# Other loads and orders of the first batches, row transposes in halves, and up1 of batch 30 behind h of batch 31, in an attention and experts kernel

## The chip, the cores and the metric

The kernel runs on one core of one Trainium2 chip. The metric is device time in microseconds (us) of one execution. Engines: PE (TensorE; PEld is its weight load), DVE (VectorE), ACT (ScalarE), POOL (GpSimd) and SP (SyncE, which here only issues DMAs).

## What is computed

Shapes: x and ctx are 32 batches of 128 channels by 1024 positions. Each batch goes through cross attention with a sliding window of 16 keys and 8 heads of 16 channels, and then, per row of 1024, through a mixture of 8 rank-64 experts of which the best two count.

```
x1  = x + Wo @ attn(q = Wq @ layernorm(x) + bq, k = Wk @ ctx + bk, v = Wv @ ctx + bv) + bo
      # position t attends to keys t-8 .. t+7
p   = softmax(layernorm(x1) @ gate_w.T); the two largest, divided by their sum -> w_full
out = x1 + sum over e of w_full[:, e] * (layernorm(x1) @ lora_A[e].T) @ lora_B[e].T
```

Rows are the 128 channels of a batch: layernorm runs along the 1024 positions, and the four projections mix channels.

## The kernel before

Weights stay in SBUF. Every operand of a large product is kept as two fp32r parts, `[:, 0]` ("hi", written by ACT) and `[:, 1]` ("lo", what is left, written by POOL or DVE), and `product` and `project_pass` (through `one_pass`, line 366) make three matmuls of them: hi-hi, hi-lo, lo-hi. Scores (line 395, 32x32 pieces), weighted values (line 416, 64x64 pieces) and transposes (line 425) are plain fp32.

The order is written out by hand for each engine: `head`, then `step` 30 times, then `tail`. A step works on several batches: `later` and `ahead` (loads, layernorm, projections of the next ones), `cur` (scores and softmax, in 4 chunks), `prev` (weighted values, output projection, residual and second layernorm) and `old` (the experts). On PE a step is, in order: project_v(cur), weighted chunk 2 of prev, 8 transposes of the normalised rows of old into the two banks of `bank_a`, score chunk 1, project_q(ahead), the down product of old in four quarters with a weighted or score chunk behind each, project_k(ahead), score chunk 3, 4 transposes of h, project_o(prev), weighted chunk 1 of cur, the up product of old in two halves (called up0 and up1 here) with score chunk 0 of ahead between.

The transposed rows are evacuated by ACT (`rows_hi`, line 718) and DVE (`rows_lo`, line 1005) in two halves, one after each four transposes. A transpose takes 128 columns of a row block and writes 128 columns of one bank:

```
for f in blocks:
    last = nc.tensor.transpose(bank[:, f * P:(f + 1) * P],
                               source[:, f * P:(f + 1) * P], ident[:])
```

`raw` is one buffer for x and ctx of a batch in turn. SP loads x into it, ACT writes the normalised x over it, POOL takes the lo part from it (`normal_lo`, line 1217), then SP loads ctx into it; ACT and POOL split that too (`context_hi`, line 723, `context_lo`, line 1194). In the head, ctx of batches 0 and 1 have places of their own (`prob_t`, `xn2`), but x of batch 1 waits for `normal_lo` of batch 0. The nine pieces of the weights are loaded in the head into buffers that are free then, and split by ACT (`split_hi`) and POOL or DVE (`split_lo`, lines 1181 and 876). The first two masks are written into `bank_b` by PE (`first_masks`, line 361), later ones by ACT (`write_mask`, line 683). `warm_up` runs 60 small matmuls ahead of all.

In the tail, batches 30 (`old`) and 31 (`last`) are finished: h transposes of 30, row transposes of 31, up of 30, down of 31, h transposes of 31, up of 31.

Of the kernel before, what the change touches and what calls it, by code (L numbers as in the profile page):

```python
# [36 lines left out]
P = 128  # L37
# [61 lines left out]
def build(nc, x, ctx, wqkvo, biases, down_w, up_w, ident_in, mask_in, consts_in, out):  # L99
    with ExitStack() as stack:  # L100
# [61 lines left out]
        weights_hi, weights_lo = sem("weights_hi"), sem("weights_lo")  # L162
# [4 lines left out]
        x_in, ctx_in = sem("x_in"), [sem("ctx_in0"), sem("ctx_in1")]  # L167
# [44 lines left out]

        def ctx_of(b):

            if isinstance(b.j, int) and b.c <= 1:
                return (prob_t[:, 0:T], xn2[:])[b.c]
            return raw[:]

        def ffn_bank(b):

            return bank_c if isinstance(b.j, int) and b.j == 0 and b.c == BATCHES - 1 else bank_a

# [28 lines left out]
        def _(sp):  # L251
# [16 lines left out]
            def load_x(b):  # L268

                row = b.row(sp)  # L270
                if b.c >= 1:
                    sp.wait_ge(xn_lo, b.count(1, 0))
                if b.c >= 3:
                    sp.wait_ge(ctx_lo, b.count(1, 0))
                sp.dma_start(raw[:], x[row]).then_inc(x_in, 16)

            def load_ctx(b):

                row = b.row(sp)
                if b.c >= 2:  # L280
                    sp.wait_ge(xn_lo, b.count(1, 1))
                sp.dma_start(ctx_of(b), ctx[row]).then_inc(ctx_in[b.parity], 16)

            def load_resid(b):
# [4 lines left out]
                else:  # L289
                    sp.wait_ge(weights_lo, 6 + b.c)  # L290
# [8 lines left out]
            def head(b0, b1, b2, b3):  # L299

                load_x(b0)
                load_ctx(b0)
                sp.dma_start(consts[:], consts_in).then_inc(consts_in_sbuf, 16)
                load_piece(0)
                load_piece(1)
                sp.dma_start(bias[:], biases).then_inc(small_in, 16)
                sp.dma_start(ident[:], ident_in).then_inc(small_in, 16)
                sp.dma_start(mask[:], mask_in).then_inc(small_in, 16)
                load_piece(2)
                load_piece(3)  # L310
                load_piece(4)
                load_piece(5)
                load_piece(6)
                load_piece(7)
                load_ctx(b1)
                load_piece(8)
                load_x(b1)
                place_v(b0)
                load_x(b2)
                load_resid(b0)  # L320
                load_ctx(b2)
# [33 lines left out]
        def _(pe):  # L355
            def first_masks():
# [3 lines left out]
                for m in range(2):  # L360
                    nc.tensor.matmul(bank_b[m][:], ident[:], mask[:], start=True, stop=False, skip_group_check=True)
# [59 lines left out]

            def transposes(bank, source, blocks):
# [15 lines left out]
            def up(b, n, e):  # L438

                last = product(ffn_bank(b)[:, n * HALF:(n + 1) * HALF], ht_split,  # L440
# [6 lines left out]
            def bank_of(b):  # L447

                return bank_a if first(b) else bank_c

            def project_q(b, free):

                pe.wait_ge(xn_done, b.count(1, 1))
                pe.wait_ge(xn_lo, b.count(1, 1))
# [871 lines left out]
```

## Time and profile before

| | us |
|---|---|
| three runs | 1031.46, 1033.31, 1034.66 |
| median | 1033.31 |
| the profiled execution | 1032.37 |
| its span, first to last instruction | 1030.6 |
| busy in the span: PE / PEld / DVE / ACT / POOL | 997.1 / 861.7 / 867.1 / 582.2 / 433.5 |
| mean granted TensorE clock, of full speed | 0.987 |

The span is what the trace covers; 1.8 us of the profiled execution lie around it. Busy times of different engines overlap. PE's matmuls are pipelined and their ends are modelled, so the distance from one group's start to the next one's start is the better measure of what it costs; the rows give starts. A granted clock of 1.0 is 2.4 GHz, 0.5 is 1.2 GHz.

### The profile page before, as it was taken

The numbers are of one execution on the slowest core, as the hardware profiler recorded it, in microseconds if no ns is written. First come the engines' busy times: TensorE is split into PE (matmuls) and PEld (weight loads), VectorE is DVE, ScalarE is ACT, GpSimd is POOL, SyncE is SP. The second block draws the span as 40 slices with busy tenths as digits, with TensorE's granted clock in tenths as the row PEclk, the third lists the DMA queues.
The fourth block names the chain that finished last, engine by engine and source line by source line (L and its number), as shares of the span: only waits on it lengthen the run. The fifth ranks groups of instructions, "written<-read, shape, count | busy, mean of one in ns | idle before, by whom it ended". The sixth has DMA issues, their size and how long they took to land.

```text
span 1030.6 us, 54778 instructions
## 1 busy us (share of the span) xinstructions
PE 997.1 (97%) x24572; PEld 861.7 (84%) x24572; DVE 867.1 (84%) x1889; ACT 582.2 (56%) x812; POOL 433.5 (42%) x373
## 2 busy tenths in 40 slices
PE   6779999999999999999999999999999999999987
PEld 5658888888888888888888888888888888888876
DVE  2778888898888898988898888889888889898872
ACT  6766555555555565555566555556555556565330
POOL 6864434343434444434444443434443434443220
PEclk8899999999999999999999999999999999999998
DMA  7323333312333322333322333331233332232211
GB/s 270 87 67 83 86 106 106 104 54 77 87 104 106 106 61 89 86 85 106 106 64 85 86 85 106 106 90 66 79 86 105 106 104 59 92 85 66 65 42 41
DMA packets 157866, 92.49 MB, mean 90 GB/s; under 512 B 139744, under 2 KB 139872, under 8 KB 157664
## 3 DMA queue, kind: packets, MB, share of 16 engines
q1 hardware_dynamic: 157664, 89.25, 29.6%
q8 instruction: 193, 3.16, 1.3%
q14 instruction: 9, 0.07, 0.0%
HBM read 55.16 MB, written 16.78 MB: 70 GB/s over the span
## 4 chain that ended last, share of the span: by engine, by line
PE 92%; DMA 2%; DVE 2%; ACT 1%; issue 1%; POOL 1%; DVEq 0%; POOLq 0%
PE bank_a L366 36%; PE bank_c L366 18%; PE bank_b L416 18%; PE bank_b L395 15%; PE bank_a L425 5%; DMA raw<-x 1%; DMA raw<-ctx 1%; DVE stats L886 0%; POOL x_split L1217 0%; POOL ctx_split L1194 0%; DVE resid_pair L1025 0%; ACT q_diag L693 0%; ACT v_sb L710 0%; ACT ctx_split L723 0%; POOL rstd L1202 0%
## 5 line engine op out<-in xcount | busy, mean ns | idle before, releaser
L416 PEld LDWEIGHTS bank_b<-prob_t,v_diag 64*64 64x64 f32 x4608 | 188.4, 133 | 33.0 <-issue 24.6
L366 PE MATMUL bank_a<-down_split,mid_split 128*128 128x264 f32 (+1 forms) x1488 | 207.6, 289 | 2.3 <-DVE mid_split L1005 2.2
L1188 POOL TENSOR_TENSOR prob<-prob,row_inv 128x512 f32<-128x512 f32 x128 | 134.3, 1050 | 169.0 <-DVE row_inv L975 169.0
L416 PE MATMUL bank_b<-prob_t,v_diag 64*64 64x96 f32 (+2 forms) x4608 | 202.6, 239 | 0.0
L366 PEld LDWEIGHTS bank_a<-down_split,mid_split 128*128 128x128 f32 x1488 | 187.6, 188 | 9.2 <-DVE mid_split L1005 2.9
L395 PEld LDWEIGHTS bank_b<-k_sb,q_diag 32*32 32x32 f32 x16384 | 155.2, 105 | 44.6 <-issue 36.5
L366 PE MATMUL bank_a<-up_split,ht_split 128*128 128x512 f32 x744 | 187.5, 401 | 0.3 <-DVE ht_split L1012 0.3
L395 PE MATMUL bank_b<-k_sb,q_diag 32*32 32x32 f32 x16384 | 170.5, 194 | 11.8 <-issue 7.7
L366 PEld LDWEIGHTS bank_a<-up_split,ht_split 128*128 128x128 f32 x744 | 135.9, 189 | 29.4 <-DVE ht_split L1012 0.7
L1211 POOL TENSOR_TENSOR attn_split<-attn,attn_split 128x1024 fp32r<-128x1024 f32 x32 | 76.1, 2377 | 139.7 <-ACT attn_split L730 139.7
L984 DVE STREAM_TRANSPOSE prob_t<-prob 128x768 f32<-128x768 f32 x128 | 121.5, 950 | 0.9 <-POOL prob L1188 0.9
L678 ACT ACTIVATE prob<-prob 128x512 f32<-128x512 f32 x128 | 80.2, 626 | 58.6 <-DVE prob L963 58.6
L672 ACT ACTIVATE attn<-bank_b,consts 128x256 f32<-128x256 f32 x128 | 59.5, 465 | 85.6 <-PE bank_b L416 85.6
L366 PE MATMUL bank_c<-ctx_split,w_split 128*128 128x512 f32 x372 | 98.5, 400 | 4.3 <-POOL ctx_split L1194 4.3
L1217 POOL TENSOR_TENSOR x_split<-raw,x_split 128x1024 fp32r<-128x1024 f32 x32 | 77.0, 2406 | 60.7 <-ACT raw L742 60.7
L1194 POOL TENSOR_TENSOR ctx_split<-raw,ctx_split 128x1024 fp32r<-128x1024 f32 x30 | 72.0, 2400 | 61.1 <-ACT ctx_split L723 61.1
L963 DVE TENSOR_TENSOR prob<-bank_b,row_max 128x512 f32<-128x512 f32 x128 | 88.5, 691 | 4.4
L957 DVE TENSOR_REDUCE row_max<-bank_b 128x16 f32<-128x512 f32 x128 | 85.0, 664 | 7.5 <-PE bank_b L395 7.2
L1202 POOL TENSOR_TENSOR rstd<-var_eps,consts 128x1 f32<-128x1 f32 x64 | 35.1, 549 | 132.1 <-DVE var_eps L895 132.1
L971 DVE TENSOR_REDUCE row_sum<-prob 128x16 f32<-128x512 f32 x128 | 85.2, 666 | 0.5 <-ACT prob L678 0.3
L905 DVE SCALAR_TENSOR_TENSOR attn<-bank_b,consts,attn 128x256 f32<-128x256 f32 x128 | 58.3, 458 | 31.2 <-ACT attn L672 31.2
L366 PEld LDWEIGHTS bank_c<-ctx_split,w_split 128*128 128x128 f32 x372 | 68.6, 191 | 17.7 <-issue 4.4
(94 smaller groups left out, 1334.4 us busy)
## 6 DMA issues: line engine op xcount, KB each, us to landing
v_diag<-v_t SPq DMA_DIRECT2D x128, 132.0 KB, 3.3
raw<-x SPq DMA_DIRECT2D x32, 512.0 KB, 5.2
resid_pair<-x SPq DMA_DIRECT2D x32, 512.0 KB, 4.8
out<-resid_pair SPq DMA_DIRECT2D x31, 512.0 KB, 2.6
raw<-ctx SPq DMA_DIRECT2D x30, 512.0 KB, 3.2
stage<-down_w SPq DMA_DIRECT2D x2, 528.0 KB, 11.4
q_diag<-up_w SPq DMA_DIRECT2D x2, 512.0 KB, 6.2
prob_t<-up_w SPq DMA_DIRECT2D x2, 512.0 KB, 8.4
```

What stands on the lines that cost most here:

```text
L366: return nc.tensor.matmul(dst, st[:, s, st_cols], mv[:, m, mv_cols], start=start and n == 0, stop=stop and n == 2)
L395: last = nc.tensor.matmul(bank_b[m % 2][rows, t * KT:(t + 1) * KT], q_diag[rows, cur.parity, n, :], keys[rows, n * QT:n * QT + KT], start= ...
L416: last = nc.tensor.matmul(bank_b[2 + m % 2][rows, lo * PW:hi * PW], value_blocks(b)[rows, n, :], prob_t[rows, at:at + (hi - lo) * KT], sta ...
L678: nc.scalar.activation(weights_of(m), weights_of(m), ACT.Exp).then_inc(exp_done, 1)
L957: nc.vector.tensor_reduce(row_max[:, cols], scores, AX_X, ALU.max).then_inc(max_done, 1)
L963: nc.vector.tensor_tensor(weights_of(m), scores, row_max[:, cols].unsqueeze(2).broadcast_to([P, CT, KT]), ALU.subtract).then_inc(shifted, 1)
L971: nc.vector.tensor_reduce(row_sum[:, cols], weights_of(m), AX_X, ALU.add).then_inc(sum_done, 1)
L984: nc.vector.transpose(prob_t[:, m * PC:(m + 1) * PC], prob[:, m % 2 * PC:(m % 2 + 1) * PC]).then_inc(prob_t_done, 1)
L1188: nc.gpsimd.tensor_tensor(weights_of(m), weights_of(m), row_inv[:, cols].unsqueeze(2).broadcast_to([P, CT, KT]), ALU.mult).then_inc(prob_d ...
L1194: nc.gpsimd.tensor_tensor(ctx_split[:, 1, :], ctx_of(b), ctx_split[:, 0, :].bitcast(F32), ALU.subtract).then_inc(ctx_lo, 1)
L1211: nc.gpsimd.tensor_tensor(attn_split[:, 1, :], attn[:], attn_split[:, 0, :].bitcast(F32), ALU.subtract).then_inc(attn_lo, 1)
L1217: nc.gpsimd.tensor_tensor(x_split[:, 1, :], raw[:], x_split[:, 0, :].bitcast(F32), ALU.subtract).then_inc(xn_lo, 1)
```

## The change

It has three parts.

**The first batches.** Batch 0's projections are single fp32 matmuls of the unsplit weights and operands (`project_first`), so no hi and lo parts are made for it; x of batch 1 is loaded into the place of `k_sb[1]`, x of batch 2 into `raw` once q of batch 0 is projected, ctx of batch 2 into `xn2`; the DMAs are issued in another order; the two first masks are written one by one; `warm_up` has 34 matmuls, and a `keep_warm` of 28 stands before score chunk 2 of batch 0; pieces 1 to 3 of the weights are split by DVE; and the orders of PE, ACT, DVE and POOL in the head differ. Semaphores of the weights' lo parts become one for each piece.

**Row transposes.** Sixteen in place of eight, each of 64 rows of `xn2` (the lower half into bank 0 of the pair, the upper into bank 1), alternating. `rows_hi` and `rows_lo` take a bank at a time, that is 64 rows of all eight blocks, ACT and DVE do both halves in a row, and the down product waits for both before its first quarter.

**Tail.** up1 of batch 30 stands behind the h transposes of batch 31; the inner parts of batch 31 go to `w_split`, so that those of batch 30 stay.

```
-                if b.c >= 1:
-                    sp.wait_ge(xn_lo, b.count(1, 0))
-                if b.c >= 3:
-                    sp.wait_ge(ctx_lo, b.count(1, 0))
-                sp.dma_start(raw[:], x[row]).then_inc(x_in, 16)
+                if early(b) and b.c == 2:
+                    sp.wait_ge(q_done, 1)
+                elif not early(b):
+                    sp.wait_ge(xn_lo, b.count(1, -1))
+                    sp.wait_ge(ctx_lo, b.count(1, -1))
+                sp.dma_start(x_of(b), x[row]).then_inc(first_x[b.c] if early(b) else x_in, 16)
...
+            def row_transposes(bank):
+
+                for f in range(FK):
+                    for z in range(HALVES):
+                        rows = slice(z * HALF_P, (z + 1) * HALF_P)
+                        at = z * HALF + f * HALF_P
+                        last = nc.tensor.transpose(bank[:, at:at + HALF_P], xn2[rows, f * P:(f + 1) * P],
+                                                   ident[rows, rows])
+                        if f == FK - 1:
+                            last.then_inc(xt_done, 1)
...
+            def project_first(bank, which, source):
+
+                for n in range(2):
+                    half = slice(n * HALF, (n + 1) * HALF)
+                    last = nc.tensor.matmul(bank[:, half], attn[:, which * P:(which + 1) * P],
+                                            source[:, half], start=True, stop=True)
+                return last
...
-                pe.wait_ge(xt_lo, old.count(2, 1))
+                pe.wait_ge(xt_lo, old.count(2, 2))
...
                 pe.wait_ge(ht_lo, old.count(1, 1))
-                for n in range(2):
-                    for e in range(EK):
-                        up(old, n, e)
+                for e in range(EK):
+                    up(old, 0, e)
                 pe.wait_ge(xt_lo, last.count(2, 2))
                 for n in range(2):
                     for f in range(FK):
                         down(last, n, f)
                 pe.wait_ge(h_done, last.count(2, 2))
                 transposes(bank_c, h_sb, range(EK)).then_inc(ht_done, 1)
+                for e in range(EK):
+                    up(old, 1, e)
                 pe.wait_ge(ht_lo, last.count(1, 1))
...
                 if old:
                     rows_lo(old, 0)
+                    rows_lo(old, 1)
                 if cur:
                     scores_shift(cur, 1)
                     weights_transpose(cur, 0)
-                if old:
-                    rows_lo(old, 1)
-                if cur:
                     weights_sum(cur, 1)
```

SP's DMAs in the head from the mask's on, before (up_w and down_w are pieces 1 to 8 of the weights, xn is `xn2`; x and ctx of batch 0 and piece 0 are issued ahead of these rows, in both kernels):

```order
L308 DMA mask<-mask_in 128x512
L254 DMA q_diag<-up_w 128x1024
L254 DMA prob_t<-up_w 128x1024 x2
L254 DMA resid_pair<-down_w 128x1024 x2
L254 DMA stage<-down_w 128x1056
L282 DMA xn<-ctx 128x1024
L254 DMA stage<-down_w 128x1056
L275 DMA raw<-x 128x1024
```

And now:

```order
L331 DMA mask<-mask_in 128x512
L275 DMA q_diag<-up_w 128x1024
L297 DMA k_sb<-x 128x1024
L306 DMA xn<-ctx 128x1024
L275 DMA q_diag<-up_w 128x1024
L275 DMA prob_t<-up_w 128x1024 x2
L275 DMA resid_pair<-down_w 128x1024
L297 DMA raw<-x 128x1024
L275 DMA resid_pair<-down_w 128x1024
L275 DMA stage<-down_w 128x1056
L286 DMA v_diag<-v_t 32x33x32 x4
L306 DMA xn<-ctx 128x1024
```

x of batch 1 stood behind all pieces of the weights, its ctx behind all but one; now both (k_sb<-x, xn<-ctx) go ahead of seven of the nine, and x of batch 2 (the second raw<-x) ahead of the last three.

PE at the start of the head, before:

```order
L496 MATMUL bank_c<-prob 32x32 x60
L361 MATMUL bank_b<-mask,ident 128x512 x2
L366 MATMUL bank_a<-ctx_split,w_split 128x512 x6
L366 MATMUL bank_c<-x_split,w_split 128x512 x6
L366 MATMUL bank_a<-ctx_split,w_split 128x512 x6
L395 MATMUL bank_b<-k_sb,q_diag 32x32 x192
L366 MATMUL bank_c<-x_split,w_split 128x512 x6
L395 MATMUL bank_b<-k_sb,q_diag 32x32 x64
```

And now (attn is the unsplit piece of the attention weights, prob_t is ctx of batch 0, raw its normalised x; L548 is `keep_warm`):

```order
L543 MATMUL bank_b<-prob 32x32 x34
L485 MATMUL bank_a<-prob_t,attn 128x512 x2
L485 MATMUL bank_c<-raw,attn 128x512 x2
L384 MATMUL bank_b<-mask,ident 128x512
L485 MATMUL bank_a<-prob_t,attn 128x512 x2
L418 MATMUL bank_b<-k_sb,q_diag 32x32 x64
L384 MATMUL bank_b<-mask,ident 128x512
L418 MATMUL bank_b<-k_sb,q_diag 32x32 x64
L548 MATMUL bank_b<-ident 32x32 x28
L418 MATMUL bank_b<-k_sb,q_diag 32x32 x64
L389 MATMUL bank_c<-x_split,w_split 128x512 x6
L418 MATMUL bank_b<-k_sb,q_diag 32x32 x64
```

The three projections of batch 0 are six instructions in place of eighteen and take no split part, and one mask stands behind the first score chunk.

PE at the end of the tail, before (bank_a is batch 30, bank_c batch 31):

```order
L425 MATMUL bank_a<-ident,h_sb 128x128 x4
L425 MATMUL bank_c<-ident,xn 128x128 x8
L366 MATMUL bank_a<-up_split,ht_split 128x512 x24
L366 MATMUL bank_c<-down_split,mid_split 128x264 x24
L366 MATMUL bank_c<-down_split,mid_split 128x256 x24
L425 MATMUL bank_c<-ident,h_sb 128x128 x4
L366 MATMUL bank_c<-up_split,ht_split 128x512 x24
```

And now:

```order
L459 MATMUL bank_a<-ident,h_sb 128x128 x4
L451 MATMUL bank_c<-ident,xn 128x64 x16
L389 MATMUL bank_a<-up_split,ht_split 128x512 x12
L389 MATMUL bank_c<-down_split,mid_split 128x264 x24
L389 MATMUL bank_c<-down_split,mid_split 128x256 x24
L459 MATMUL bank_c<-ident,h_sb 128x128 x4
L389 MATMUL bank_a<-up_split,ht_split 128x512 x12
L389 MATMUL bank_c<-up_split,w_split 128x512 x24
```

Twelve of the 24 matmuls of up of batch 30 stand between the h transposes and the up product of batch 31, which reads its stationary operand from w_split.

## Rows read from the trace of the kernel before

**Rows 1.** The page: busy time, share of the span and instructions of each engine

```profile
PE 997.1 (97%) x24572; PEld 861.7 (84%) x24572; DVE 867.1 (84%) x1889; ACT 582.2 (56%) x812; POOL 433.5 (42%) x373
```

**Rows 2.** Windows: from:to, length, busy by engine, PEclk (granted clock), DMA share, GB/s

```profile
150.00:950.00 800.00, 798.71 (x20005) 692.23 (x20005) 707.68 (x1540) 466.50 (x652) 334.21 (x287) 1.00 0.31 88
1021.00:1022.00 1.00, 1.00 (x4) 0.79 (x3) 0.00 (x0) 0.00 (x0) 0.00 (x0) 0.50 0.00 0
```

**Rows 3.** Timeline of PE, one steady step: start, length, instructions

```profile
500.93 1.56 PE L366 MATMUL bank_c<-ctx_split,w_split 128*128 128x512 f32 x6
502.42 1.58 PE L416 MATMUL bank_b<-prob_t,v_diag 64*64 64x64 f32 x36
503.92 1.09 PE L425 MATMUL bank_a<-ident,xn 128*128 128x128 f32 x8
504.94 1.41 PE L395 MATMUL bank_b<-k_sb,q_diag 32*32 32x32 f32 x128
...
507.79 1.61 PE L366 MATMUL bank_a<-down_split,mid_split 128*128 128x264 f32 x12
...
521.03 0.66 PE L425 MATMUL bank_a<-ident,h_sb 128*128 128x128 f32 x4
521.44 1.63 PE L366 MATMUL bank_c<-attn_split,w_split 128*128 128x512 f32 x6
...
528.67 3.01 PE L366 MATMUL bank_a<-up_split,ht_split 128*128 128x512 f32 x12
531.53 1.56 PE L366 MATMUL bank_c<-ctx_split,w_split 128*128 128x512 f32 x6
```

**Rows 4.** Groups by form: busy us, mean ns of one, idle before

```profile
L416 PEld LDWEIGHTS bank_b<-prob_t,v_diag 64*64 64x64 f32 x4608 | 188.4, 133 | 33.0 <-issue 24.6
...
L366 PEld LDWEIGHTS bank_c<-ctx_split,w_split 128*128 128x128 f32 x372 | 68.6, 191 | 17.7 <-issue 4.4
...
L425 PEld LDWEIGHTS bank_a<-ident,xn 128*128 128x128 f32 x248 | 26.5, 140 | 1.6 <-ACT xn L749 0.4
```

**Rows 5.** Timeline of DVE in that step, first lo part of the transposed rows

```profile
505.82 0.65 DVE L1005 TENSOR_TENSOR mid_split<-bank_a,mid_split 128x512 fp32r<-128x512 f32 x1
```

**Rows 6.** Timeline of PE, head and start of the first step

```profile
9.58 1.96 PE L361 MATMUL bank_b<-mask,ident 128*128 128x512 f32 x4 [1.27 <-DMA mask<-mask_in]
...
12.79 1.63 PE L366 MATMUL bank_c<-x_split,w_split 128*128 128x512 f32 x6
...
19.67 2.99 PE L395 MATMUL bank_b<-k_sb,q_diag 32*32 32x32 f32 x207 [1.06 <-ACT q_diag L693]
...
29.80 2.21 PE L366 MATMUL bank_c<-x_split,w_split 128*128 128x512 f32 x6
...
58.90 2.90 PE L366 MATMUL bank_c<-ctx_split,w_split 128*128 128x512 f32 x6 [4.32 <-POOL ctx_split L1194]
...
68.34 1.66 PE L366 MATMUL bank_c<-ctx_split,w_split 128*128 128x512 f32 x6
```

**Rows 7.** Chain that ended last, in order of time, first 80 us

```profile
10.30 2.40 POOL x_split L1217
...
12.72 9.05 DMA raw<-x
```

**Rows 8.** Timeline of DVE, head: lo part of the attention weights

```profile
7.99 2.05 DVE L876 TENSOR_TENSOR w_split<-attn,w_split 128x512 fp32r<-128x512 f32 x1 [1.72 <-ACT w_split L655]
```

**Rows 9.** Timeline of ACT, head

```profile
7.87 1.23 ACT L742 ACTIVATE x_split<-raw,shift,rstd 128x1024 fp32r<-128x1024 f32 x1
...
17.23 2.29 ACT L693 ACTIVATE q_diag<-bank_c,bq_scaled,consts 128x1024 f32<-128x1024 f32 x2
19.41 1.12 ACT L710 ACTIVATE v_sb<-bank_a,bias 128x1024 f32<-128x1024 f32 x1
```

**Rows 10.** Timeline of PE, end of the tail

```profile
1017.98 0.66 PE L425 MATMUL bank_c<-ident,h_sb 128*128 128x128 f32 x4 [0.58 <-DVE h_sb L946]
1020.05 7.32 PE L366 MATMUL bank_c<-up_split,ht_split 128*128 128x512 f32 x24 [1.41 <-DVE ht_split L1012]
```

More of the change, by code:

```diff
@@ L161, in build @@
         weights_in = [sem(f"weights_in{n}") for n in range(9)]
[L162 removed]
+        weights_hi = sem("weights_hi")
+        weights_lo = [sem(f"weights_lo{n}") for n in range(9)]
         bq_ready = sem("bq_ready")
@@ L355, in _, with first_mask @@
         def _(pe):
-            def first_masks():
+            def first_mask(m):
                 pe.wait_ge(pads_zero, 7)
                 pe.wait_ge(small_in, 16 * 3)
-                for m in range(2):
-                    nc.tensor.matmul(bank_b[m][:], ident[:], mask[:], start=True, stop=False, skip_group_check=True)
+                nc.tensor.matmul(bank_b[m][:], ident[:], mask[:], start=True, stop=False, skip_group_check=True)
             def one_pass(n, dst, st, st_cols, mv, mv_cols, start, stop):
@@ L495, in warm_up, with keep_warm @@
                 for n in range(matmuls):
-                    nc.tensor.matmul(bank_c[0:KT, 0:KT], prob[:, 0:KT], prob[:, 0:KT], start=True, stop=True)
+                    nc.tensor.matmul(bank_b[2][0:KT, 0:KT], prob[:, 0:KT], prob[:, 0:KT], start=True, stop=True)
+            def keep_warm(matmuls):
+                for n in range(matmuls):
+                    nc.tensor.matmul(bank_b[2][0:KT, 0:KT], ident[:, 0:KT], ident[:, 0:KT], start=True, stop=True)
             def head(b0, b1, b2, b3):
-                warm_up(60)
-                first_masks()
+                warm_up(34)
                 project_k(b0, None)
                 project_q(b0, None)
+                first_mask(0)
                 project_v(b0, (k_out, b0.count(1, 1)))
@@ L740, in normalise_x @@
                 act.wait_ge(shift1, later.count(1, 1))
-                for target in (x_split[:, 0, :], raw[:]):
-                    last = nc.scalar.activation(target, raw[:], ACT.Identity, bias=shift[:, 0:1],
+                for target in ((x_of(later),) if first(later) else (x_split[:, 0, :], x_of(later))):
+                    last = nc.scalar.activation(target, x_of(later), ACT.Identity, bias=shift[:, 0:1],
                                                 scale=rstd[:, 0:1])
@@ L1034, in first_norm @@
             def first_norm(later):
-                dve.wait_ge(x_in, later.count(16, 16))
-                layernorm_stats(0, raw, ln1_step, later)
+                if early(later):
+                    dve.wait_ge(first_x[later.c], 16)
+                    if later.c >= 1:
+                        dve.wait_ge(shift1, later.c)
+                else:
+                    dve.wait_ge(x_in, later.count(16, -32))
+                layernorm_stats(0, x_of(later), ln1_step, later)
             def head(b0, b1, b2, b3):
```

253 lines of the change are left out of this document (137 added, 116 removed).

## The prediction

> **What bounds the kernel now.** I read the page first, then the windows, then PE's timeline. The page has PE busy in 97% of the span, the next engine, DVE, in 84% [rows 1]. In the window from 150 to 950 us PE is busy 798.71 of 800 us at a granted clock of 1.00 [rows 2]: the middle of the run is PE's own work, and only fewer PE cycles shorten it. One step lasts from 500.93 to 531.53, 30.60 us [rows 3], and there are 30 of them. DVE's 707.68 us in the same window are 27 us a step [rows 2], so DVE follows as long as a step stays above that.
>
> The ends are different. In the head PE waits: 4.32 us on the lo part of a ctx at 58.90, for instance, and the first step begins only at 68.34 [rows 6]. From 9.58, where the first masks run, to 68.34 there are 9 projections, 9 score chunks and 6 weighted chunks of work. At a steady step's prices these are 1.49, about 1.36 (2.85 from the scores at 504.94 to the down product at 507.79, less one projection of 1.49) and 1.50 [rows 3]: 13.4 + 12.2 + 9.0 = 34.6 us. With 1.4 us for the masks, from 9.58 to about 11.0, where I take the first projection to begin [rows 6], the head loses about 58.8 - 36.0 = 22.8 us. In the tail PE waits 1.41 us at 1020.05 for the split of h of batch 31 [rows 10], and the clock granted just behind it is 0.50 [rows 2], its lower level of 1.2 GHz.
>
> **Part 1, row transposes.** Today eight transposes take 503.92 to 504.94, 1.02 us [rows 3]. The four transposes of h take 521.03 to 521.44, 0.41 us, so one costs about 0.107 of streaming (128 columns) and about 0.16 us of the 1.02 are the changes of tile shape at both ends. The change issues sixteen, in eight pairs that use different halves of the array's rows and different banks, each with 64 moving columns. No row shows a pair of 64x128 tiles. The nearest is the weighted chunk: 36 matmuls of 64x64 tiles in 1.50 us [rows 3], that is 18 pairs at 83 ns with 85 columns on average (768 columns in 9 pairs, each column streamed in two instructions), so pairs of 64 rows do run side by side there. If they do here, a pair streams 64 columns in half of 0.107, 0.053 us, plus 0 to 0.013 of overhead as in the weighted chunk: 8 x 0.053 to 8 x 0.066 + 0.16 = 0.58 to 0.69 us. Saving 0.33 to 0.44 us; I take 0.40.
>
> It counts where PE is the bound: in the 30 steps. In the tail the transposes of batch 30 are followed by a wait for the evacuation, and those of batch 31 stand beside the split of h of batch 30, for which PE waits anyway, so I count nothing there. Sum: 30 x 0.40 = 12.0 us.
>
> What moves with it: the down product now waits for both evacuated halves. DVE does the first lo part from 505.82, 0.65 us [rows 5], and would do the second right behind it, to 507.12; its hi part on ACT is ready by then, since all transposes end at 504.5 and two hi parts of about the same length follow. PE reaches the down product at 507.79 today and at 507.39 then: no wait, with 0.27 us to spare. DVE's score shift and its transposition of weights start 0.65 later, which the lo part missing behind them gives back. ACT splits ctx 0.6 later, with most of a step until its projection. I cost these at nothing: PE's next chunks cover them. If the spare 0.27 us were gone, PE would wait a tenth or two in each step.
>
> The weight load is the other side. Loads of 64 and 128 columns take 133 and 191 ns, those of the transposes, with 128 columns, 140 [rows 4]: 58 ns per 64 columns, and about 7 + 58 = 65 ns for a transpose's 128 columns if the same fixed part is taken off. Every one of the sixteen loads still has 128 columns, so twice as much is loaded as now. Side by side, 65 ns per pair hides behind or equals the streaming; one behind the other it is 130 per pair, 8 x 0.130 + 0.16 = 1.20 us, 0.18 more than today. Here the Trainium skill speaks, "TensorE: Matmul & The Clock Gate", section on LDWEIGHTS: a load's time scales with its columns and not with its rows, and 128 columns of 32 rows cost as much as of 128 rows. By that rule the change halves no load. The same page, Part 3, says that loads and matmuls of different row groups overlap, which gives the saving above; no run here shows either for this shape.
>
> **Part 2, the head.** I replay PE with the durations of the trace. Batch 0 loses two splits from its path: the lo part of the attention weights, ready at 10.04 [rows 8], and that of its x, ready at 12.70 [rows 7], behind which q started at 12.79 [rows 6]. A projection becomes four fp32 instructions of 512 columns. The four of the two masks took 1.4 us from 9.58 and are pipelined, and four times 128 columns at 0.107 are 0.43, so I take 0.43 each, 1.7 us in place of 1.49: 0.6 us more for three. x is normalised at 7.87 + 1.23 = 9.1 today [rows 9] and without the split of ctx ahead of it at about 8.5, q is projected by 10.3, ACT has split a piece by 11.0 and places q in 2.29 us [rows 9]: scores at about 13.4 in place of 19.67 [rows 6]. The larger piece is batch 1. Its x was issued at 12.72 because it needed `raw`, and took 9.05 us to land behind the weights [rows 7]. Now three large loads are ahead of it; it should land some 9 us after its issue near 4.5, at the latest 13.5, where it landed at 21.8. Then ACT's order decides: from 13.3 on the evacuation of v (1.12 [rows 9]), two splits as long, an exponential of half as many columns (0.6) and two normalisations of 1.23 end at 19.7; POOL's lo part of 2.40 [rows 7] ends at 22.1, and q of batch 1 starts there in place of at 29.80 [rows 6]: 7.7 earlier. From there x of batch 2 and ctx of batch 2 are there in time, and the wait of 4.32 us at 58.90 has no cause any more; the six matmuls behind it, 2.90 us long in place of 1.49 [rows 6], should be as short as in a steady step, 1.4 us. That is 7.7 + 4.3 + 1.4 = 13.4 us, less 0.5 to 2.5 because DVE now splits three more pieces: the one lo part that it does today took 2.05 us for 512 columns [rows 8], while POOL was busy. I take 12.0, the first step at about 56.3. As bounds: 8 if only batch 1's lead of 7.7 is kept, 15 if the order leaves PE nothing but its own waits for place_v.
>
> **Part 3, the tail.** up1 of batch 30 costs 2.86 us from 528.67 to 531.53 [rows 3] and is only moved. The split of h of batch 31 needs 1018.4 to 1020.05, 1.65 us, and is now covered by it: the 1.41 us of idle go [rows 10]. The 24 matmuls behind took 7.32 us by their group's length, at twice 2.86 plus the 0.16 by which such a group overhangs they take 5.9, so the clock cost 1.4; most of it goes too, since PE doesn't stop. I take 2.5 in all, bounds 1.4 and 2.8. The last store starts as much earlier.
>
> **The sum.** 12.0 + 12.0 + 2.5 = 26.5 us off the profiled execution's 1032.37 gives 1005.9; the median of the runs is 0.9 above that execution, so I say **1006**.
>
> **The rivals.**
> (a) *Pairs run one behind the other, or their loads do.* The eight pairs take 1.0 to 1.2 us instead of 0.6 and part 1 gives nothing or costs up to 0.18 x 30 = 5.4 us. For it: doubled loads. Against it: 64-row pairs overlap in the weighted chunks, though there each half also has its own columns. Time: 1032.4 - 12 - 2.5 + (0 to 5.4) = 1018 to 1023, taken as 1019.
> (b) *The head gives a third.* POOL and DVE are the chain there; if DVE's added splits each wait for a POOL instruction of 2.40 us [rows 7], three of them put 7 us back onto the chain, and the head gives 5: 1032.4 - 12 - 5 - 2.5 = 1013.
> (c) *Slower.* A 64-row transpose load runs at the ordinary rate of 58 ns per 64 columns, 116 for its 128, and the two of a pair don't overlap: 16 x 0.116 + 0.16 = 2.0 us, 1.0 more than now, 30 us in all, 1048 with parts 2 and 3 kept. The point from which this makes the kernel slower is 1.02 + 14.5/30 = 1.5 us for the sixteen. For it: row 4's ordinary loads and doubled count. Against it: 18 pairs of 64-column loads in 1.50 us are 83 ns per pair, less than the 116 that two such loads would take one behind the other.
> (d) *The change does not do what it says*, PE waiting at the down product for the second half by what the transposes saved: that gives (a)'s time by another way, and its rows would be a stall of 0.4 us on mid_split in each step.
>
> **How the numbers follow.** Forecast 0.62; (a) with (d) 0.20; (b) 0.10; (c) 0.08. 0.3% of this time, 3 us, is about what can be told from no change. The forecast's own range is 1032.4 - 13.2 - 15 - 2.8 = 1001 to 1032.4 - 9.9 - 8 - 1.4 = 1013. The range from 999 to 1021 holds it, (b) and most of (a). Faster by over 3 us: 0.62 + 0.19 + 0.10 = 0.91; slower: (c) less its mild end, 0.06; within 3 us: 0.03.
>
> **What would show it.** In PE's timeline of a step the sixteen transposes take 0.6 to 0.7 us and the step 30.2; the first step starts at 54 to 58; in the tail no wait for h of batch 31 longer than 0.1 us and no clock of 0.50 behind it. I would be wrong by part 1 if the sixteen take 1.0 us or more or if PE waits for mid_split, and by part 2 if q of batch 1 starts later than 25.

## The result, and the profile after

The changed kernel is slower: a median of 1058.93 us (four runs, 1056.57 to 1062.11) against 1033.17 us for the kernel before on the same chip, a ratio of 1.025 with a 95% interval of 1.022 to 1.028. The prediction of 1006 us, its range and its sign were wrong. The profiled execution took 1060.9 us, its span 1059.0. All profiles and ratios are of fast runs; one of the seven runs of e1_whole (below) was a slow one, 2331.69 us, and is left out, so its median is 1026.97 where the seven give 1027.64.

The page after: PE's busy time, a score group of part 5 (its last column is PE's idle time before it and what ended most of it) and the DMA queues.

```profile
PE 997.6 (94%) x24826; PEld 857.6 (81%) x24826; DVE 874.0 (83%) x1892; ACT 580.3 (55%) x810; POOL 421.9 (40%) x368
...
L418 PE MATMUL bank_b<-k_sb,q_diag 32*32 32x32 f32 x16384 | 173.1, 194 | 36.1 <-issue 34.7
...
q8 instruction: 195, 3.19, 1.2%
```

PE is busy as long as before [rows 1], in a span 28.4 us longer. 34.7 us of waits stand before score matmuls and are put down to "issue": PE waited for nothing that the profile shows as a semaphore. Before, that row had 7.7.

Windows of the kernel after, columns as in [rows 2]:

```profile
150.00:950.00 800.00, 767.85 (x19306) 663.14 (x19304) 684.22 (x1484) 447.24 (x625) 320.15 (x277) 0.99 0.30 86
343.00:344.00 1.00, 1.00 (x13) 0.94 (x11) 0.96 (x4) 0.00 (x0) 0.00 (x0) 0.50 0.00 0
```

In the window where PE was busy 798.71 us before, it is now busy 767.85. The second row lies behind a wait of 1.68 us: the granted clock is down to 0.50.

PE's timeline, one step without such a wait, to be held against [rows 3]:

```profile
518.04 1.56 PE L389 MATMUL bank_c<-ctx_split,w_split 128*128 128x512 f32 x6
519.53 1.58 PE L439 MATMUL bank_b<-prob_t,v_diag 64*64 64x64 f32 x36
521.03 0.71 PE L451 MATMUL bank_a<-ident,xn 64*128 64x64 f32 x16
521.67 1.29 PE L418 MATMUL bank_b<-k_sb,q_diag 32*32 32x32 f32 x128
522.89 1.67 PE L389 MATMUL bank_c<-x_split,w_split 128*128 128x512 f32 x6
524.39 1.60 PE L389 MATMUL bank_a<-down_split,mid_split 128*128 128x264 f32 x12
...
548.16 1.56 PE L389 MATMUL bank_c<-ctx_split,w_split 128*128 128x512 f32 x6
```

The sixteen transposes take 0.64 us from start to start, the down product does not wait, and the step takes 30.12 us against 30.60. Steps differ a little in turn: from transposes to transposes they take 30.18 and 30.13 us (490.85 to 551.16), before 30.60 and 30.48 (503.92 to 565.00), so an undisturbed step gains 0.39 us on average. That is as predicted; but the average of the 30 steps, from the transposes at 71.09 to those at 1021.22, is 31.67 us.

Head and tail after, for [rows 6] and [rows 10]:

```profile
15.92 1.28 PE L418 MATMUL bank_b<-k_sb,q_diag 32*32 32x32 f32 x128
...
21.66 1.82 PE L418 MATMUL bank_b<-k_sb,q_diag 32*32 32x32 f32 x119 [3.20 <-issue]
...
25.39 2.72 PE L548 MATMUL bank_b<-ident 128*32 128x32 f32 x47 [1.29 <-issue]
...
30.49 0.61 PE L418 MATMUL bank_b<-k_sb,q_diag 32*32 32x32 f32 x47 [1.44 <-issue]
31.08 2.29 PE L389 MATMUL bank_c<-x_split,w_split 128*128 128x512 f32 x6
...
54.14 1.39 PE L418 MATMUL bank_b<-k_sb,q_diag 32*32 32x32 f32 x85 [2.59 <-issue]
...
67.98 1.67 PE L389 MATMUL bank_c<-ctx_split,w_split 128*128 128x512 f32 x6
...
1047.40 2.99 PE L389 MATMUL bank_a<-up_split,ht_split 128*128 128x512 f32 x12
1050.23 5.60 PE L389 MATMUL bank_c<-up_split,w_split 128*128 128x512 f32 x24
```

The first step starts at 67.98 (68.34 before): the head gave 0.4 us. The tail is as foretold: no wait for the split of h of batch 31, and the 24 matmuls take 5.60 us in place of 7.32.

**Where the waits stand.** I numbered PE's instructions in program order: an fp32 matmul is four (two loads and two matmuls in the trace), an fp32r matmul or a transpose two, and where a group waits for two or three semaphores one instruction only waits. A score chunk has 256. The trace has 49,407 of them before and 49,920 after. The page's row of the instruction queue counts 195 packets of 16 KiB after (above), and on the page of the kernel before:

```profile
q8 instruction: 193, 3.16, 1.3%
```

That is one packet per 256 instructions in both. The 32 issue waits of 0.3 us or more in the steps after (33.6 us together) and those of the head stand, to one or two instructions, at number 195 past a multiple of 256, so a block of instructions is counted from there. (Before, the steps have three such waits, 1.7 us together.) A step had 1536 instructions before, 6 x 256, so the blocks began at the same places in every step: score chunks 0 to 3 started 77, 203, 81 and 215 instructions into a block. The change adds eight transposes, 16 instructions: 1552. The blocks now drift through the step, and most waits come where a block holds much of a score chunk. One of them, on PE's timeline, and the instruction queue in the DMA view's window from 150 to 151 us:

```profile
149.65 1.55 PE L389 MATMUL bank_c<-ctx_split,w_split 128*128 128x512 f32 x6
151.13 1.24 PE L418 MATMUL bank_b<-k_sb,q_diag 32*32 32x32 f32 x123
153.21 0.25 PE L418 MATMUL bank_b<-k_sb,q_diag 32*32 32x32 f32 x5 [0.84 <-issue]
```

```profile
q8 instruction: 1, 0.02, 5.8%
```

This block began behind the first of the six projection matmuls, near 149.9; PE ran out of it at 152.37, after 2.5 us, and went on at 153.21. The packet with the next one started at 150.86 (by narrowing the window) and took 0.93 us (5.8% of 16 engines in 1 us). So PE had the next block 3.3 us after it had begun this one. Over the 39 such waits of the changed kernel's head and steps PE went on 2.1 to 3.0 us after the packet's start (once 3.3), and 2.1 to 5.6 us after it had begun the block, 16 of them between 3.3 and 4.3. Nor did it begin any other block sooner than 2.1 us after its packet's start. In the kernel before, the blocks of a step lasted 4.4, 3.7, 6.7, 3.4, 4.9 and 7.5 us, which was nearly always enough.

So theory F, as the expectations call it: PE gets its instructions in blocks of 256, one packet each, and waits where it runs through 256 sooner than the next block comes. (That the packet is asked for when the block before is begun is an inference; the trace shows only when it starts.) Its rivals blame the pairs of 64 rows or the new orders of the other engines.

### The profile page after: what moved, and what is told of

The parts are those of the page before. It is cut to its first block, busy times and chain, and to the rows that moved or that the text cites. A ratio compares the mean times of both kernels' runs of the same rounds, so it can differ in the third digit from the quotient of the medians.

```text
span 1059.0 us, 55265 instructions
## 1 busy us (share of the span) xinstructions
PE 997.6 (94%) x24826; PEld 857.6 (81%) x24826; DVE 874.0 (83%) x1892; ACT 580.3 (55%) x810; POOL 421.9 (40%) x368
## 3 DMA queue, kind: packets, MB, share of 16 engines
q8 instruction: 195, 3.19, 1.2%
## 4 chain that ended last, share of the span: by engine, by line
PE 91%; issue 5%; DVE 2%; POOL 1%; ACT 1%; DMA 1%; SPq 0%; DVEq 0%; POOLq 0%
PE bank_a L389 36%; PE bank_b L439 18%; PE bank_c L389 17%; PE bank_b L418 15%; PE bank_a L459 2%; PE bank_a L451 2%; DMA prob_t<-ctx 1%; POOL down_split L1240 0%; PE bank_a L485 0%; PE bank_b L548 0%; DVE mid_split L1059 0%; DVE stats L940 0%; POOL x_split L1278 0%; ACT q_diag L743 0%; DVE prob_t L1038 0%
## 5 line engine op out<-in xcount | busy, mean ns | idle before, releaser
L439 PEld LDWEIGHTS bank_b<-prob_t,v_diag 64*64 64x64 f32 x4608 | 192.1, 135 | 35.8 <-issue 27.6
L389 PE MATMUL bank_a<-down_split,mid_split 128*128 128x264 f32 (+1 forms) x1488 | 209.9, 290 | 6.7 <-issue 3.4
L439 PE MATMUL bank_b<-prob_t,v_diag 64*64 64x96 f32 (+2 forms) x4608 | 207.2, 241 | 2.7 <-issue 2.6
L418 PE MATMUL bank_b<-k_sb,q_diag 32*32 32x32 f32 x16384 | 173.1, 194 | 36.1 <-issue 34.7
L1278 POOL TENSOR_TENSOR x_split<-raw,x_split 128x1024 fp32r<-128x1024 f32 x30 | 72.2, 2407 | 81.9 <-ACT raw L798 81.9
L1253 POOL TENSOR_TENSOR ctx_split<-raw,ctx_split 128x1024 fp32r<-128x1024 f32 x29 | 69.5, 2397 | 73.0 <-ACT ctx_split L779 73.0
L389 PE MATMUL bank_c<-ctx_split,w_split 128*128 128x512 f32 x372 | 96.8, 395 | 0.0
```

The lines of the kernel that those rows point to most:

```text
L389: return nc.tensor.matmul(dst, st[:, s, st_cols], mv[:, m, mv_cols], start=start and n == 0, stop=stop and n == 2)
L418: last = nc.tensor.matmul(bank_b[m % 2][rows, t * KT:(t + 1) * KT], q_diag[rows, cur.parity, n, :], keys[rows, n * QT:n * QT + KT], start= ...
L439: last = nc.tensor.matmul(bank_b[2 + m % 2][rows, lo * PW:hi * PW], value_blocks(b)[rows, n, :], prob_t[rows, at:at + (hi - lo) * KT], sta ...
L1253: nc.gpsimd.tensor_tensor(ctx_split[:, 1, :], ctx_of(b), ctx_split[:, 0, :].bitcast(F32), ALU.subtract).then_inc(ctx_lo, 1)
L1278: nc.gpsimd.tensor_tensor(x_split[:, 1, :], x_of(later), x_split[:, 0, :].bitcast(F32), ALU.subtract).then_inc(xn_lo, 1)
```

## The experiments

All times are medians in us; kernels before ran beside each set (1031.4 to 1032.6), and the ratios are to those. In e5_less16 the output lacks some scores; the others compute all of it.

| run | what | steps' instructions | time | ratio, 95% |
|---|---|---|---|---|
| e1_whole | changed, part 1 undone | 1536 | 1026.97 | 0.992-0.997 |
| e2_pad16 | before, 16 instructions more a step | 1552 | 1093.95 | 1.057-1.064 |
| e3_pad64_once | before, 64 more once | 1536 | 1081.72 | 1.043-1.052 |
| e4_pad240 | changed, 240 more a step | 1792 | 1512.05 | 1.459-1.469 |
| e5_less16 | changed, 16 fewer a step | 1536 | 1011.12 | 0.979-0.986 |
| e6_split | changed, score chunks cut | 1552 | 1036.63 | 1.005-1.011 |
| e7_tail | before with part 3 | 1536 | 1028.68 | 0.996-0.999 |
| e8_split_head | e6 and a shorter head | 1552 | 1032.17 | 1.000-1.003 |
| e9_mixed_early | 4 of 8 transposes in pairs, fewer waits | 1536 | 1025.78 | 0.993-0.997 |
| e10_head | e9 moved by 124 | 1536 | 1054.69 | 1.018-1.024 |
| e11_early | changed, fewer waits | 1544 | 1040.25 | 1.005-1.010 |
| e12_alternate | pairs in every second batch | 1544, 1528 | 1023.59 | 0.991-0.994 |

**e1_whole** takes part 1 back.

```
-                row_transposes(bank_a)
+                transposes(bank_a, xn2, range(0, 4)).then_inc(xt_done, 1)
+                transposes(bank_a, xn2, range(4, FK)).then_inc(xt_done, 1)
```

> The changed kernel with the row transposes of before (eight of 128 columns, evacuated as before); head and tail as changed. PE then issues 1536 instructions a step, six times 256, as before the change, in place of 1552. Theory F (PE waits for its own instructions at every 256th one, 194 or 195 past a multiple, when the 256 ahead of it were used up in less than about 2.4 us): the steps are 30.6 us again without waits, the head gives about 0.4 and the tail about 3.5, so 1029 us. Rival S (the new head or its loads slow the steps, the transposes are innocent): about 1050. Rival T (the transposes of 64 rows or the later start of the down product cause the waits by themselves): 1029 too; the next kernel tells it from F.

1026.97: part 1, which saves time in each undisturbed step, costs 32 us in all, and the other two parts gain 6 (3.6 to 8.6 by the interval). The rival that blames the head or its loads, about 1050, is out.

**e2_pad16, e3_pad64_once** leave the work of the kernel before alone and add only waits for a semaphore that was reached long ago, two to an instruction.

```
+                for _ in range(32):     # e2: each step, behind the transposes
+                    pe.wait_ge(pads_zero, 1)
...
+                for _ in range(128):    # e3: once, in the head
+                    pe.wait_ge(pads_zero, 1)
```

> The kernel before with 32 waits on a semaphore that has long been reached behind the row transposes of each step, which are 16 instructions of PE: 1552 a step, no other change, all matmuls as before. Theory F: waits of 0.3 to 2 us for which no engine is the reason, at every 256th instruction where it falls near a score chunk, some 25 to 35 us over the run: 1060 us, and a step without such a wait stays 30.6. Rivals S and T: 1033 to 1036, no such waits but the few of before.

> The kernel before with 128 waits on a reached semaphore, 64 instructions of PE, once, in the head where PE waits 4.3 us anyway. A step stays 1536 instructions, so the places of the boundaries stay fixed, but 64 instructions away from where they were: score chunks 1 and 3, or 2 and 0, start within 30 of a boundary in every step. Theory F: one or two waits of about 1 us in each of the 30 steps, so 1060 to 1095 us. Without F: 1033 to 1036, since 64 instructions are issued once in idle time.

The score rows of e2_pad16 and e3_pad64_once:

```profile
L395 PE MATMUL bank_b<-k_sb,q_diag 32*32 32x32 f32 x16384 | 175.6, 194 | 44.3 <-issue 36.7 <-ACT bank_b L685 4.1 <-ACT q_diag L695 1.6
```

```profile
L395 PE MATMUL bank_b<-k_sb,q_diag 32*32 32x32 f32 x16384 | 179.7, 194 | 47.7 <-issue 42.9 <-ACT bank_b L685 3.2 <-ACT q_diag L695 1.6
```

e3 decides it. 64 instructions once, in the head, cost 49 us. Some 5 of them fall in the head itself, whose first row transposes start at 76.67 in place of 71.80; the rest is in the steps, where 56 issue waits of 0.3 us or more add up to 37.9 us: the blocks of all later steps lie elsewhere against the work, and two places of nearly every step wait from there on. No pair, no other order and no more instructions per step are in it.

e2 was foretold at 1060 and took 1093.95, so it missed by more than half of the loss, though its waits are there: 34.4 us in the steps, at the same number 195. The 16 instructions also cost some 0.2 us a step where they stand (1.20 to 1.25 us from the transposes to the score chunk in most steps, before 1.02), 6 us in all. The rest isn't accounted for.

**e4_pad240** makes the changed kernel's step 7 x 256 with waits.

> The changed kernel with 480 waits on a reached semaphore a step, 240 instructions, spread over ten places between score chunks 1, 2 and 3: 1792 a step, seven times 256, and 14 fewer matmuls of keep_warm so that chunks 1 to 3 start about 148 past a boundary. More instructions, but none of the boundaries drifts. Theory F, with added instructions that cost PE nothing: steps of 30.2 us without waits, 1021 to 1027 us in all. If an added instruction costs 10 ns or more of PE's time, 2.4 us a step more, 1095. Rival T: still the waits of the changed kernel, 1059 or more.

```
+            def pad(waits):
+                for _ in range(waits):
+                    pe.wait_ge(pads_zero, 1)
```

No remedy, and far from both numbers set down: 453 us more for 240 x 30 instructions is 63 ns for each. Its idle times mostly stand behind the added waits, up to 2.5 us at a time, not at number 195, so it tests neither theory F nor its rival.

**e5_less16** keeps the pairs and drops one tile of scores, `if t == left_out: continue`, for chunk 1 of a step.

> The changed kernel with the four score matmuls of one tile (tile 7 of chunk 1) left out in each step, so its output lacks the scores of these tiles; everything else, the pairs of 64 rows too, is as changed. The step is again 1536 TensorE instructions, 6 blocks of 256, and the score chunks start where they did before in their blocks. Theory F (TensorE is fed in blocks of 256 instructions and waits where a block coincides with a score chunk): the waits put down to issue fall from 46 us to under 15, and the time is about 1014 us (e1_whole's 1027.6, less 0.38 us x 30 for the pairs, less 0.08 us x 30 for the matmuls left out), 1011 to 1019. Rival G (the pairs of 64 rows, or the new order of the parts on ScalarE and VectorE, make the waits): the waits stay, about 1056 us, the changed kernel less 2.

Its score row, and its window:

```profile
L420 PE MATMUL bank_b<-k_sb,q_diag 32*32 32x32 f32 x16144 | 165.6, 194 | 10.4 <-issue 9.1
```

```profile
150.00:950.00 800.00, 798.75 (x20248) 689.71 (x20248) 718.66 (x1558) 473.15 (x664) 335.88 (x289) 1.00 0.32 89
```

1011.12, within 3 of the 1014 set down, and no issue wait of 0.3 us or more in the first 29 steps: what is left of the 9.1 is in the head. Its undisturbed steps take 30.05 and 30.18 us in turn. With 16 instructions fewer the same pairs gain what part 1 promised, and the rival that blames the pairs or the other engines' order (about 1056) is out.

**e6_split, e8_split_head** cut chunks in two, so that no block is all scores.

```
-                    scores_chunk(cur, 1)
+                    scores_chunk(cur, 1, range(8))
                 if ahead:
                     project_q(ahead, (v_out, cur.count(1, 1)))
+                if cur:
+                    scores_chunk(cur, 1, range(8, CT))
```

> The changed kernel, 1552 instructions a step as it is, whole output, with the score chunks 1 to 3 of a step cut in two pieces around matmuls that were beside them (8 tiles before and 8 behind the query projection; 12 before and 4 behind four down products; 3 before and 13 behind the rest of the down products and the key projection). By theory F no 256 instructions in a row are then issued in under some 2.4 us, whatever the position of the block, and the issue waits of the steady steps go though the step is no multiple of 256: 1013 to 1019 us. By rival G, or if only steps of 6 x 256 instructions run without waits, the waits stay and the time is 1055 to 1060.

> e6_split with two edits in the head: the 28 small matmuls that keep the clock up (112 instructions) are four wide ones (16 instructions), and the query projection of batch 2 stands between the last two score chunks of batch 1 instead of behind them. By theory F the head's waits of 1.29 and 1.44 us (blocks that hold the small matmuls) and 2.59 us (three chunks in a row) become smaller: 2 to 5 us less than e6_split. If the head is bound by its loads and not by instructions: the same as e6_split within 1 us.

The waits of the steps went but for five, 2.9 us together (the score row has 9.2 us of issue, most of it in the head), though the step is no multiple of 256; but the time came down only to 1036.63, where 1013 to 1019 had been set down. PE's timeline of e6_split shows why:

```profile
504.76 0.75 PE L418 MATMUL bank_b<-k_sb,q_diag 32*32 32x32 f32 x64
505.44 1.67 PE L389 MATMUL bank_c<-x_split,w_split 128*128 128x512 f32 x6
507.04 0.83 PE L418 MATMUL bank_b<-k_sb,q_diag 32*32 32x32 f32 x64
507.80 1.71 PE L389 MATMUL bank_a<-down_split,mid_split 128*128 128x264 f32 x12
```

From 504.76 to 507.80 are 3.04 us where the whole chunk and the projection took 2.72 (521.67 to 524.39 above). The step is 30.69 to 30.77 us with three cuts, 0.5 to 0.6 more than uncut: 0.2 us a cut, 0.3 for the one shown. Every piece more has two changes of tile shape, to which I put it down. I had costed these at nothing. In e8 the first down product waits until 74.58, in e6 until 74.64: the head's edits did not bring the steps forward, and what the 4 us between the two medians are is open.

**e7_tail** is part 3 by itself: 2.5 us less (0.6 to 4.2).

> The kernel before with part 3 alone (the last up products in another order, inner parts of the last batch in the freed weights). The steps keep 1536 instructions. Expected: the tail gives 2.5 to 3.5 us and nothing else moves, 1029 to 1031 us against 1032.6. If the order of the tail makes waits elsewhere: 1033 or more.

**e9_mixed_early, e10_head, e11_early.** Two edits give back 16 instructions without dropping work: half of the blocks as wholes, and waits put on matmuls of the group ahead.

```
+            def spread(left):
+                if early and left <= len(early):
+                    pe.wait_ge(*early.pop(0))
```

> The changed kernel with whole output and steps of 1536 TensorE instructions again. Two edits. Only 4 of the 8 transposed blocks go as pairs of 64 rows, 4 as wholes (12 transposes, 24 instructions, where there are 32); and where TensorE waits for two or three semaphores ahead of a group of matmuls, all but one of the waits stand on the last matmuls of the group before, which takes away the 8 instructions per step that only wait. By theory F: no issue waits in the steady steps, and 1027.6 (e1_whole) less half of the pairs' gain (0.19 us x 30 = 5.7), about 1022 us, and less by what 8 instructions that only wait cost a step: nothing if they are hidden, up to 0.07 us each (e4_pad240), 17 us in all; so 1005 to 1022. If only the count of instructions in the head, the loads or the order of the parts mattered, the waits would stay: 1040 or more.

> e9_mixed_early with the head's 28 small matmuls that keep the clock up as 2 wide ones and 5 fewer warm-up matmuls: 124 TensorE instructions fewer once, so the score chunks 1 to 3 start 87, 219 and 95 instructions into a block where they start 211, 87 and 219 in e9_mixed_early, both clear of the stretch that made waits. By theory F the steady steps stay free of waits and the head loses one block of 256 in two: 0 to 3 us less than e9_mixed_early. If the position of the blocks mattered in another way than I think, the steady steps would wait again: 20 us more or worse.

> The changed kernel with all pairs of 64 rows and only the waits moved onto the matmuls before, which takes 8 instructions from each step: 1544, which drifts by 8 a step through the blocks where the changed kernel drifts by 16. By theory F the score chunks pass the bad stretch at half the speed and half as often, so the issue waits come to about the same sum as in the changed kernel (35 to 46 us), in fewer and longer runs of steps: about 1055 us less what the 8 instructions cost (0 to 17): 1038 to 1059. If instead each instruction above 1536 costs time by itself, half of the loss goes: about 1035. If the pairs were slow by themselves: 1059.

e9 is without waits in the steps but for one (1.15 us), and its 1025.78 us lie above the 1005 to 1022 that I had put down. The 8 waiting instructions had cost next to nothing: undisturbed steps of e11, which lacks them, mostly take 30.09 and 30.13 us, those of the changed kernel 30.13 and 30.18. The step of e9 is 30.57 us on average, as long as before: its four pairs and four whole transposes take 0.97 us together, where eight whole ones take 1.02 and eight pairs 0.64. And the score chunk behind whole transposes takes 1.34 us in every second step, in e9 as before, and 1.22 in the others; behind eight pairs it takes 1.22 wherever no issue wait falls into it. Why the mixture gains so little is open.

e10 refutes the number that I had used, some 2.4 us for a block. Timeline of PE in e10_head, and its DMA rows from 526 to 527 and from 527 to 528 us:

```profile
525.98 1.29 PE L441 MATMUL bank_b<-k_sb,q_diag 32*32 32x32 f32 x128
527.20 1.69 PE L409 MATMUL bank_a<-down_split,mid_split 128*128 128x256 f32 x12
528.82 0.49 PE L463 MATMUL bank_b<-prob_t,v_diag 64*64 64x64 f32 x6
530.26 0.96 PE L463 MATMUL bank_b<-prob_t,v_diag 64*64 64x96 f32 x18 [0.95 <-issue]
```

```profile
q1 hardware_dynamic: 100, 0.38, 96.8%
...
q1 hardware_dynamic: 50, 0.14, 34.7%
q8 instruction: 1, 0.02, 6.0%
```

The block is 219 instructions of score chunk 2, a down group and 12 of the weighted chunk, from 526.15 to 529.31: 3.16 us, more than 2.4. But the next came only at 530.26, 4.1 us after 526.15; its packet started at 527.95, with the queues busy at 96.8% until 527 and at 34.7% behind. So my expectation had its length wrong: I had read it from waits alone, without the time that the block before had lasted.

Nor would another length do. In e9 a block of 3.3 us stands in every step without a wait, in e10 26 waits stand in the steps, mostly behind blocks of 3.2 to 3.3. What differs is the packet's start: 0.2 to 1.0 us before PE begins that block in e9, mostly 1.1 to 2.4 us behind the block's beginning in e10. The changed kernel has the extremes. Five of its 32 waits end blocks of 4.3 to 4.9 us, whose packets started 2.5 to 2.9 us late, and this score chunk is a block nearly to itself, 1.3 us long, without a wait behind it:

```profile
421.04 1.29 PE L418 MATMUL bank_b<-k_sb,q_diag 32*32 32x32 f32 x128
422.26 3.01 PE L389 MATMUL bank_a<-up_split,ht_split 128*128 128x512 f32 x12
```

The packet with the instructions from 422.3 on started at 418.45, 2.6 us before PE began the chunk. Data transfers are not needed for a late packet: the one of 247.60, 2.8 us late, and that of 418.45 both lie in stretches with no data transfer. What sets the packet's start is open.

e11 drifts at half the speed and by F should have waited as long as the changed kernel in all; it has 23.4 us of issue in its score row against 34.7, and its 1040.25 us lie at the lower end of the 1038 to 1059 set down. Places and drift fit F, the size did not come out of it.

**e12_alternate** goes by pairs in every second batch, with the moved waits of e11.

```
+        def in_pairs(b):
+            return b.parity == 1
```

> The kernel of e11_early with the pairs of 64 rows in every second batch and whole transposes in the others, whole output: steps of 1544 and 1528 TensorE instructions in turn, 3072 = 12 x 256 for two, so the score chunks move forth and back by 8 instructions and stay 203 to 219 (chunks 1 and 3) and 79 to 87 (chunk 2) instructions into a block. By theory F there are no issue waits in the steady steps. A step with pairs is 0.48 us shorter than one without (30.12 against 30.60; in e9_mixed_early the four pairs gave but 0.03, as the score chunk that comes behind a whole transpose is 0.13 us longer), so half of 0.48 x 30 = 7.2 us, less 0.03 x 30: about 6 us below e9_mixed_early, 1018 to 1021. If only an exact multiple of 256 in every step keeps the waits away: 1030 or more.

1023.59, a ratio of 0.9925 (0.991 to 0.994), with one issue wait (0.91 us) in the steps though their instructions are 1544 and 1528: the best kernel with whole output, 8 us below the kernel before, and 3 above the 1018 to 1021 that I expected. The expectation counted 0.48 us for a step with pairs. But the pairs stand in the steps whose score chunk takes 1.22 us anyway, and the whole transposes in those where it takes 1.34 to 1.37, so only the 0.38 of the transposes is gained; pairs in the other batches, which would also save the 0.12, were not run.

## Why the prediction was wrong

**What bounds the kernel.** Right as far as it went: PE's own work. But the trace of before had 7.7 us of issue waits in its score row, and I did not ask what feeds PE.

**Part 1, the transposes: right in size.** Foretold 0.58 to 0.69 us for the sixteen, measured 0.64. The pairs overlap, loads included; rival (a), 1.0 to 1.2 us, and rival (c), 2.0, are refuted. The undisturbed step gains 0.39 us, against 0.40 foretold (the 0.48 in the expectation of e12_alternate compares a long step of before with a short one of after). The transposes give 0.38 of it. The score chunk behind them gives another 0.06 on average: it takes 1.22 us in every step, and behind whole transposes 1.35 in every second one (505.65 to 507.00 in e1_whole), which is also the 0.12 by which the steps of before differ. Some 0.05 is lost elsewhere.

The Trainium skill, "TensorE: Matmul & The Clock Gate", section on LDWEIGHTS, has a load's time go by its columns; here no load of the pairs became shorter, 138 ns against 140 before. By Part 3 of the same page of the Trainium skill loads and matmuls of different row groups overlap. The trace agrees: 0.64 us, where loads one behind the other would have made the 1.20 us of the prediction.

**"I cost these at nothing: PE's next chunks cover them": right.** No wait for mid_split in the steady steps, so rival (d) is out too. The exceptions are the first step (1.64 us; before 1.02 and 1.16) and one near the end (1.19).

**The failing step is the sum itself.** It priced the sixteen new instructions by their streaming and had no term for their number, nor for how PE's instructions reach it. From transposes to transposes the 30 steps took 950.1 us (71.09 to 1021.22), before 917.3 (71.80 to 989.08). 30 x 0.39 = 11.7 us were gained, and the waits for blocks rose from 1.7 to 33.6. That leaves some 13 us more behind the waits. Up to half of it is the clock: four waits of 1.50 to 1.97 us (that of 341.64, for one) are followed by some 3 us at a granted clock of 0.50, and the steps that hold them are 1.7 to 1.9 us longer than an undisturbed step and its waits. The other steps with waits are 0.2 to 0.8 us longer so; why is open, and e3_pad64_once shows the like, with the clock at 1.00 in all its steps (963.0 us, of which 37.9 are waits). The forecast's slower rival had another mechanism, so its 0.08 was no cover. (A slip beside it: 1005.9 and 0.9 are 1006.8, not 1006.)

The Trainium skill, "Runtime: NRT & Kernel Launch", section "Instruction fetch mechanics", says that engines refill their instruction memory in blocks of 16 KiB, 256 instructions, and that crossing into a block is mostly hidden. The 16 KiB and the 256 agree with the q8 row (195 packets, 3.19 MB, for 49,920 instructions). Hidden it is in nearly every step of the kernel before, where the blocks last 3.4 us or more; in the changed kernel it was not, and cost 33.6 us of waits.

**Part 2, the head: wrong. Foretold 12.0, got about nothing.** In the profile the first step starts 0.4 us earlier. By the medians, e1_whole's 6 less e7_tail's 2.5 leave 3.6 to part 2, with an interval that takes in zero. I started q of batch 1 as soon as its operand would be ready, at 22.1. POOL finished that operand at 24.1 (a lo part of 2.35 us from 21.78), but q started at 31.08, later than the 25 that I had named as a sign of being wrong: PE works in order, and score chunks 1 and 2 and 28 small matmuls are ahead of it. These are short instructions in great number: the block that PE began at 16.0 lasted until 18.5, the packet of the next started at 19.47, and PE went on at 21.66, 5.6 us after 16.0. `keep_warm` alone adds 112 instructions. The issue waits of the head add up to 10.9 us, against 5.6 before.

**Part 3, the tail: right.** 2.5 foretold; 2.5 (0.6 to 4.2) by e7_tail, 3.5 in the changed kernel's profile.

What stays open: what sets the packet's start, from 2.6 us before PE begins the block ahead to 2.9 us after in the steps; the time lost behind the waits that neither they nor the clock hold; and the head's gain by itself, which no run separates.

## What to carry to other kernels

Where an engine runs hundreds of tiny instructions (a score chunk's 256 in 1.22 us here), count its instructions per loop step and where each block of 256 begins: a step that is a multiple of 256 holds its position, good (e1_whole) or bad (e3_pad64_once), for the whole run, one that is not sweeps through the bad ones, and an edit of 64 instructions in the head can cost more than the edit under test gains. An "issue" wait that comes back at a fixed distance in instructions is a fetch, and the instruction queue's packets in the DMA view show when it started. How long a block lasts doesn't tell by itself whether PE will wait; the packet's start does. Compare variants at the same position of the blocks.

## What the runs showed of the hardware

PE's instructions come in packets of 256, one packet a block (193 for 49,407, 195 for 49,920). PE begins no block sooner than 2.1 us after its packet starts, and where it waits goes on 2.1 to 3.0 us after (150.86 to 153.21, 527.95 to 530.26, 19.47 to 21.66), once 3.3. In the changed kernel's steps the packet starts 2.6 us before to 2.9 us after PE begins the block ahead, with no data transfer at either end. An instruction that only waits costs 63 ns of PE in rows of many (e4_pad240), and next to nothing alone: eight fewer a step make it 0.04 us shorter (e11_early). A cut of a score chunk costs 0.2 to 0.3 us (e6_split). Pairs of 64x128 fp32 transposes in different row halves and banks run side by side, 0.64 us for eight pairs.
